# Where ScalarE's list holds the exponentials of batches 0, 1 and 2: ahead of the centring of h and of the normalisation of x

## The reference, cut to what matters

```python
h = _layernorm(x) * (1 + ca) + sa
scores = jnp.where(mask, q @ k, 0.0) / scale     # mask: offsets 0, 1, 2, 4 ... 256 back
attn = softmax(scores)                            # masked places still count exp(0)
x = x + ga * (attn @ v @ Wo.T + bo)
h = _layernorm(x) * (1 + cb) + sb
x = x + gb * (mx_quantize(h) @ mx_quantize(W).T + bias)
```

## Time and profile before

| | |
|---|---|
| time, median of 3 runs | 286.92 us (286.64 to 287.34) |
| the profiled execution's own time | 286.72 us |
| its span | 285.0 us |
| busy share: PE, DVE, ACT, POOL | 90%, 91%, 75%, 74% |
| TensorE's granted clock over the span | 1.0 |

### The profile page before, as it was taken

The page is one execution under the profiler, slowest core; times in us unless marked ns, Lnnn a source line. Parts: engine busy times, 40 slices in busy tenths (PEclk is TensorE's granted clock), DMA queues, the critical chain, the costliest instruction groups (busy, mean ns, idle before and its releaser), DMA issues.

```text
span 285.0 us, 4442 instructions
## 1 busy us (share of the span) xinstructions
PE 255.6 (90%) x1368; PEld 158.8 (56%) x1368; DVE 258.8 (91%) x326; ACT 212.5 (75%) x577; POOL 210.5 (74%) x152
## 2 busy tenths in 40 slices
PE   6999997697978795989999999999999988997885
PEld 1653554175526561666556646664567646794663
DVE  3699799969995999999999999999999999999970
ACT  2386987975697779879898989887776937575752
POOL 7101439895879999999999999999999699845100
PEclk9999999999999999999999999999999999999999
DMA  7743977694784239724993389347943965730005
GB/s 225 193 181 81 340 248 232 230 338 133 240 273 148 73 125 350 251 72 131 295 336 127 129 263 286 135 113 222 333 147 94 279 198 178 230 103 11 0 26 199
DMA packets 54399, 53.91 MB, mean 189 GB/s; under 512 B 4100, under 2 KB 52824, under 8 KB 54376
## 3 DMA queue, kind: packets, MB, share of 16 engines
q1 hardware_dynamic: 54376, 53.63, 60.1%
HBM read 44.90 MB, written 8.72 MB: 188 GB/s over the span
## 4 chain that ended last, share of the span: by engine, by line
DVE 39%; POOL 19%; PE 18%; issue 11%; ACT 11%; DVEq 0%; POOLq 0%; ACTq 0%
POOL pv_buf L677 14%; DVE prod L1721 9%; DVE pv_buf L1851 9%; DVE prod L1851 4%; DVE prod L1710 4%; PE ps L988 3%; PE ps L1067 3%; PE ps L826 2%; ACT dump L1197 2%; PE ps L853 2%; ACT dump L1238 1%; DVE ps L1825 1%; PE ps L837 1%; DVE ps L1827 1%; POOL rstd L658 1%
## 5 line engine op out<-in xcount | busy, mean ns | idle before, releaser
L677 POOL TENSOR_TENSOR pv_buf<-pv_buf 128x1024 f32<-128x1024 f32 (+2 forms) x60 | 132.5, 2209 | 15.0 <-DVE pv_buf L1851 9.8
L1721 DVE TENSOR_TENSOR prod<-ps,kT 128x1024 f32<-128x1024 f32 (+4 forms) x70 | 75.1, 1110 | 0.0
L1851 DVE TENSOR_TENSOR pv_buf<-v_shift,ps 128x1024 f32<-128x1024 f32 x49 | 59.1, 1212 | 0.0
L937 PE MATMUL ps<-prod,sel_sum 128*32 128x512 f32 x256 | 30.8, 598 | 8.5 <-DVE prod L1721 7.8
L853 PE MATMUL ps<-wT,h_cen 128*128 128x256 f32 x128 | 29.9, 379 | 0.0
L826 PE MATMUL ps<-hT,wT 128*128 128x512 f32 x64 | 29.7, 596 | 0.0
L837 PE MATMUL ps<-hT,wT 128*128 128x512 f32 x64 | 29.3, 599 | 0.0
L988 PE MATMUL ps<-wo_g,w_raw 128*128 128x256 f32 x112 | 27.9, 392 | 0.0
L853 PEld LDWEIGHTS ps<-wT,h_cen 128*128 128x128 f32 x128 | 23.9, 190 | 6.4 <-issue 3.8
L988 PEld LDWEIGHTS ps<-wo_g,w_raw 128*128 128x128 f32 x112 | 20.1, 189 | 5.4 <-issue 3.2
L937 PEld LDWEIGHTS ps<-prod,sel_sum 128*32 128x32 f32 x256 | 6.7, 109 | 28.0 <-issue 13.8
(11 more groups left out here) (212 smaller groups left out, 550.3 us busy)
## 6 DMA issues: line engine op xcount, KB each, us to landing
v_shift<-v_rows SPq DMA_DIRECT2D x56, 512.0 KB, 5.7
x_in<-in_L_attn_x SPq DMA_DIRECT2D x8, 512.0 KB, 4.4
v_rows<-v_base SPq DMA_DIRECT2D x8, 512.0 KB, 4.1
x_res<-in_L_attn_x SPq DMA_DIRECT2D x8, 512.0 KB, 6.5
out_x<-outb SPq DMA_DIRECT2D x5, 512.0 KB, 5.8
rows_mod<-mod_rows SPq DMA_DIRECT2D x7, 256.0 KB, 3.4
x<-in_L_wmod SPq DMA_DIRECT2D x1, 1024.0 KB, 7.9
row_ga<-mod_rows SPq DMA_DIRECT2D x8, 128.0 KB, 4.9
```

The lines of the kernel that those rows point to most:

```text
L677: nc.gpsimd.tensor_tensor(dst, dst, ring(b, n)[:, t:NT, :], ALU.add).then_inc(s_add, 1)
L937: mm = nc.tensor.matmul(ps23[32 * g:32 * g + 32, 1, :], sel_sum[:, which, c, :], prod[:, n, c, :], start=(c == 0 and which == 0), stop=(c ...
L1721: nc.vector.tensor_tensor(prod[:, n, :, o:L], ps01[:, :, o:L], kT[:, b % 2, :, 0:L - o], ALU.mult).then_inc(s_prod, 1)
L1851: nc.vector.tensor_tensor(dst[:, t:NT, :].rearrange("p t (h e) -> p t h e", e=DH), v_n.rearrange("p t (h e) -> p t h e", e=DH), weights, A ...
```

## The change

Three blocks of ScalarE's list move behind a softmax's exponentials. `centre_h(1)` now follows `exps(0)`. `norm_before(3)`, which ended iteration 0, follows `exps(1)` and `mean_of_v(0)` in iteration 1. `norm_before(4)`, which ended iteration 1, follows `exps(2)` and `mean_of_v(1)` in iteration 2, ahead of `norm_after(0)`. `norm_before(5)` and later ones stay where they were. No instruction is added or removed, and no other engine's list changes.

```diff
             seed_q(1)
-            centre_h(1)
 
             for b in range(LAST - 1):
                 ahead, norm1 = has(b + 2), has(b + 3)
                 exps(b)
+                if b == 0:
+                    centre_h(1)
                 if has(b - 1):
                     mean_of_v(b - 1)
+                if 0 < b < TAIL - 1:
+                    norm_before(b + 2)
...
                 if has(b + 2):
                     seed_q(b + 2)
-                if has(b + 3):
+                if b >= TAIL - 2 and has(b + 3):
                     norm_before(b + 3)
-                elif has(b - 1):
+                elif b >= TAIL - 2 and has(b - 1):
                     norm_after(b - 1)
```

## The result

| | before | after |
|---|---|---|
| median | 286.93 us (286.64 to 287.34) | 291.42 us (288.58 to 291.85) |
| ratio | 1 | 1.0142, 95% interval 1.0083 to 1.0202 |
| mean granted clock of the executions | 1.0 in the profiled one | 0.953 to 0.974 |
| profiled execution | 286.72 us, span 285.0 | 288.58 us, span 286.9 |

Slower by 1.4%, where the prediction had 0.2% faster. The profiled execution of after is the fastest of its kind; the others took 291.3 us and more at a clock of 0.953 to 0.959, and a fifth on record 291.92 us. The page already shows what the prediction had nowhere: TensorE's granted clock, in tenths, over 40 slices of 7.2 us. It is lower near 90, 118 and 222 us.

The account below looks back on a forecast made before the run. VectorE was taken to hang on GpSimd through ScalarE, with GpSimd gapless behind 95 us. GpSimd's 0.73 us gain less 0.16 for the later norm_after(0) gave -0.57 us: median 286.92 to 286.35 us, range 285.4 to 287.2.

Parts of the forecast that it names:

- VectorE's stops, 4.92 us: Between maxima and weights of batches 0 to 2, shorter waits for ScalarE's exponentials save VectorE 1.08 + 1.98 + 1.86 us.
- ScalarE's 0.42 us, GpSimd's 0.73: Iteration 0: centring behind the exponentials delays ScalarE 0.42 us; GpSimd's sixth add of batch 0 still comes 0.73 us earlier.
- The second norm behind the moved one: Iteration 2: norm_after(0) waits behind exponentials and norm of batch 4, costing 0.16 us; first modulation 0.57 us earlier, at 94.50.
- TensorE, which runs from the same transposes.: Iteration 1: ScalarE's list up to batch 2's score copies is unchanged, so the maxima of batch 2 start 0.73 us earlier.
- past this all four engines hang on one another with the same shift: Behind the weights of batch 3, lists are the same, so GpSimd's 0.57 us lead carries to the end.
- The rivals: Whole wait won, 282.0 or 284.7 us (6%); smaller ScalarE delay, 286.0 (16%); slower, 287.1 or 287.5 (14%); nothing, 286.9 (9%).
- The slower one: Moved norm of batch 4 makes norm_after(0) late for GpSimd: 287.1 or 287.5 us; 14%, over 0.3% slower in 9%.
- The range: Forecast interval for the changed kernel's median, 285.4 to 287.2 us, leaving out the whole wait won and the far slower end.

Follow-up runs that it names:

- after_late: Changed kernel with TensorE's larger gaps in batches 0 to 3 filled by 256-column full matmuls, plus a few late ones: median 288.31 us, ratio 1.0030 to the kernel before.
- centre_only: Kernel before with only the centring of h of batch 1 moved behind the exponentials of batch 0: median 290.17 us.
- centre_norm3: Kernel before with centring and norm of batch 3 moved, norm of batch 4 left; run only filled: ratio 0.9950 with early and late full matmuls.
- busy_all: Changed kernel with small matmuls (3 rows, 512 columns) ahead of the turned scores: 2, 8 and 3 for batches 1, 2, 3; median 291.27 us.
- busy_two: Changed kernel with 8 small matmuls (3 rows, 512 columns) ahead of the turned scores of batch 2 alone: median 288.57 us.
- centre_norm3_dense: Kernel before with centring and norm of batch 3 moved, norm of batch 4 left, filled with 1, 5 and 3 full matmuls: median 290.01 us.
- after_one: Changed kernel with only four 256-column full matmuls added, ahead of the turned scores of batch 2: median 290.07 us, ratio 1.0073 to the kernel before.
- norm3_only: Kernel before with only the norm of batch 3 moved behind the exponentials of batch 1: median 289.65 us.
- norm3_dense: Kernel before with only the norm of batch 3 moved, plus 5 and 3 full matmuls ahead of the scores of batches 2 and 3: median 290.15 us.
- before_dense: Kernel before with one full matmul added ahead of the turned scores of batch 2: median 287.65 us.
- before_late: Kernel before with TensorE's larger gaps in batches 0 to 3 filled by 256-column full matmuls, plus a few late ones: median 287.29 us, ratio 1.0024 to it unfilled.
- dense_all: Changed kernel with 1, 5 and 2 full matmuls (128 rows, 512 columns) ahead of the turned scores of batches 1, 2, 3: median 292.06 us.

## Why the prediction was wrong, point by point

- **VectorE's stops, 4.92 us.** Right: 0.21 us is left of each, and TensorE's scores of batch 2 took most of it back (2.97 us of waiting; some 2.5 forecast, and 2.70 in after_late at clock 1.0).
- **ScalarE's 0.42 us, GpSimd's 0.73.** Right: the rstd of batch 2 at 41.29 after the start-up is taken off, the sixth add without a wait. centre_only has 0.71 us at the modulation.
- **The second norm behind the moved one.** Right, and the dearest part of the change: GpSimd waits 1.76 us for it. Without that move (centre_norm3) 2.03 us are kept instead of 0.52.
- **"TensorE, which runs from the same transposes."** This step failed, and with it "past this all four engines hang on one another with the same shift". The prediction gave TensorE's matmuls the same length in both orders. It computed that VectorE would be 2 us ahead and the scores late, so that TensorE no longer waits 1.81 us at the head sums, but it never asked what else changes with that: the wait ahead of the scores became 2.19 us, the clock fell to 0.50, the q rows took 1.4 us longer, and 2.1 longer in batch 3. So the weights of batch 3 came at 120.74 us without a wait for ScalarE, since VectorE had waited 1.75 us for TensorE's scores instead. The term for the clock was missing altogether; its size is 291.42 us against 286.67 at clock 1.0, 4.7 us in the usual execution and 1.9 in the best. That the clock costs this is shown; that the gathered piece makes it fall isn't, see below.
- **The rivals.** None had this mechanism. The slower one was by a late second norm, at most 287.5; its price was right (6.70 us from the maxima of batch 2 to the modulation; after has 95.30 - 88.61 = 6.69), the loss was elsewhere. A slower end was given 9%.
- **The range** had nothing in it for the clock. The 3 executions of before known then took 286.64 to 287.34 us, none of them dear; of 123, 35 were. That the measured time lies outside it therefore doesn't speak against the steps up to the first modulation.
- **Open:** what makes the clock fall more often in the new order. Gathered idle time isn't enough of an answer: centre_only fell behind two pieces of 1.81 and 0.72 us, after near 222 us behind hardly any idle time, and before went through pieces of 2.07 (at 44 us) and 2.77 us (at 54 us) at clock 1.0. One thing in the record points at iteration 0: with the centring moved TensorE idles 2.48 us at 45 us instead of 2.07, and clocks of 0.953 were seen only in kernels with the centring moved and that gap unfilled (after, busy_all, busy_two, centre_only), though not in all of them: centre_norm3_dense and after_one stop at 0.965; norm3_only went to 0.963, the 123 executions of before to 0.964. But norm3_dense fell there behind 2.07 us, so the length alone doesn't decide, and no run fills this gap alone. Open too is why the executions of one kernel differ, with the same gaps: before_dense filled one and changed nothing, before_late filled the larger ones and kept 5 of 12 dear executions.

## What to carry to other kernels

When a change lets one engine run ahead, ask as well what TensorE does in the time, since its clock isn't a constant: here a lower clock cost more than the waits removed gave. Check the granted clock of several executions of the kernel before, since a kernel at full clock in its profile may be near the edge. And of several moves toward one goal, look for the one that puts work ahead of what a saturated engine waits for: with the other two moves alone 2.03 us were kept up to the modulation, with all three 0.52.

## What the runs showed of the hardware that was not expected

- In after an idle piece of 2.19 us behind one-column matmuls was followed by half the clock; the two pieces of 1.81 and 0.71 us were at clock 1.0 in before, and the same two were followed by half the clock in centre_only (q rows of 5.36 us). Near 222 us the clock of after fell with TensorE busy 1.89 of the 2 us ahead.
- Executions at a mean clock of 0.986 to 0.994 were no slower in the kernel before; at 0.953 the changed kernel was 4.7 us slower than at 1.0 with its gaps filled.
- Behind eight matmuls of 3 rows and 512 columns, 1.90 us long, the clock fell in busy_two (0.65 from 87 to 91 us); behind matmuls of 128 rows in the same place it stayed at 1.00 in dense_all, after_one and after_late.
- A float32 matmul of 128 by 512 shows as two records and took 0.9 us (4.54 us for five), one of 256 columns 0.49 (1.97 us for four).
- The start-up ahead of the first maxima differs by up to 1.3 us between profiles (31.4 to 32.7 us), more than the order is worth.
